# Transformer stack on one core: value products of two key tiles joined, two-bank maxima, shared semaphore clears

## The reference, cut to what matters

```
# first attention (causal, ReLU instead of softmax)
scores = einsum('bhqd,bhkd->bhqk', q, k) / sqrt(D)
att = relu(scores) * tril(ones)
att = att / (sum(att, -1) + 1e-9)
ctx = einsum('bhqk,bhkd->bhqd', att, v)
...
# second attention, beside the experts
attn = softmax(einsum('bqhd,bkhd->bhqk', q, k) / sqrt(hd), -1)
attn_out = einsum('bhqk,bkhd->bqhd', attn, v)
return attn_out + moe_out
```

## Time and profile before

| | us |
|---|---|
| median of three runs | 2062.03 |
| the profiled execution | 2057.7 |
| span of that execution (first to last instruction) | 2055.7 |
| first attention, line 885 first to last start | 324.3 to 514.9 |
| second attention, first maximum matmul to the end | 1573.7 to 2055.7 |

### The profile page before, as it was taken

The page is one execution under the profiler, slowest core; times in us unless marked ns, Lnnn a source line. Parts: engine busy times, 40 slices in busy tenths (PEclk is TensorE's granted clock), DMA queues, the critical chain, the costliest instruction groups (busy, mean ns, idle before and its releaser), DMA issues. The chain is left out here.

```text
span 2055.7 us, 36446 instructions
## 1 busy us (share of the span) xinstructions
PE 1875.9 (91%) x10746; PEld 1173.4 (57%) x10746; DVE 1491.7 (73%) x4145; ACT 937.9 (46%) x2116; POOL 981.3 (48%) x1657
## 2 busy tenths in 40 slices
PE   6997998999899999799998798799797999999997
PEld 5885773333688888577776332688573233333332
DVE  3334896777477777699997587677666889988981
ACT  1112564556122212444443344455451477777777
POOL 3554564555333333233332111388545666666662
PEclk9998998999899999999999898799997799999999
DMA  4331668786100000893000200277765444443320
GB/s 136 116 115 32 166 168 205 153 169 126 47 1 1 1 1 1 326 413 158 1 1 3 65 10 11 60 183 197 205 209 141 94 97 100 100 104 92 91 60 27
DMA packets 241226, 215.01 MB, mean 105 GB/s; under 512 B 117210, under 2 KB 215548, under 8 KB 240924
## 3 DMA queue, kind: packets, MB, share of 16 engines
q1 hardware_dynamic: 231404, 186.56, 34.3%
q0 software_dynamic: 9648, 26.36, 4.0%
HBM read 108.04 MB, written 103.12 MB: 103 GB/s over the span
## 5 line engine op out<-in xcount | busy, mean ns | idle before, releaser
L3051 DVE TENSOR_REDUCE attend_mx<-ps 128x1 f32<-128x512 f32 x512 | 321.0, 681 | 37.0 <-PE ps L2705 33.2
L2848 ACT ACTIVATE attend_w<-ps 128x512 f32<-128x512 f32 x512 | 280.6, 597 | 95.0 <-PE ps L2719 87.3
L2705 PE MATMUL ps<-keep_x,keep_o 96*128 96x512 bf16 x512 | 209.0, 414 | 6.3 <-DVE attend_mx L3051 4.5
L2719 PE MATMUL ps<-keep_o,keep_x 99*128 99x512 bf16 x512 | 191.5, 383 | 2.7 <-ACT attend_w L2848 2.7
L2705 PEld LDWEIGHTS ps<-keep_x,keep_o 96*128 96x128 bf16 x512 | 50.1, 98 | 192.2 <-DVE attend_mx L3051 145.5
L981 POOL TENSOR_TENSOR keep_early<-keep_early,first_causal 128x128 f32<-128x128 f32 x256 | 113.3, 458 | 86.0 <-ACT keep_early L949 85.0
L1003 DVE SCALAR_TENSOR_TENSOR keep_early<-ps,first_causal 128x512 f32<-128x512 f32 (+3 forms) x256 | 113.8, 485 | 47.4 <-PE ps L885 43.1
L949 ACT ACTIVATE keep_early<-ps 128x512 f32<-128x512 f32 (+3 forms) x256 | 98.7, 437 | 85.1 <-PE ps L885 84.9
L1216 PE MATMUL ps<-mlp_zT,keep_early 128*128 128x128 f32 x1056 | 129.2, 282 | 8.0 <-ACT mlp_zT L1258 8.0
L2737 PE MATMUL ps<-attend_w,keep_early 128*17 128x512 f32 x1024 | 135.5, 598 | 0.0
L1216 PEld LDWEIGHTS ps<-mlp_zT,keep_early 128*128 128x128 f32 x1056 | 122.9, 195 | 16.0 <-ACT mlp_zT L1258 16.0
(11 more groups left out here) (399 smaller groups left out, 4406.7 us busy)
## 6 DMA issues: line engine op xcount, KB each, us to landing
sorted<-keep_x SPq DMA_DIRECT2D x3, 14720.0 KB, 75.1
tok_xin<-in_xk SPq DMA_DIRECT2D x64, 256.0 KB, 2.6
qk_parts<-qkv_parts SPq DMA_DIRECT2D x33, 384.0 KB, 3.2
qk_parts<-moe_parts SPq DMA_DIRECT2D x32, 384.0 KB
sorted<-moe_zn POOLq DMA_DIRECT2D x69, 128.0 KB, 2.5
keep_o<-qk_parts SPq DMA_DIRECT2D x16, 384.0 KB, 4.5
keep_x<-qk_parts SPq DMA_DIRECT2D x16, 384.0 KB, 5.6
moe_zs<-sorted SPq DMA_DIRECT2D x45, 128.0 KB, 2.5
```

The costliest lines, as they stand in the source:

```text
L2705: nc.tensor.matmul(ps[:, MX + i % RING, :], qs[0:R, x.buf(0), h, t * P:(t + 1) * P], ks[0:R, x.buf(0), h, :], start=True, stop=True).then_ ...
L2719: nc.tensor.matmul(ps[:, SC + i % RING, :], ks[:, x.buf(2), HG * g + j, kt * P:(kt + 1) * P], qs[:, x.buf(2), HG * g + j, :], start=True, ...
L2848: nc.scalar.activation(w[:, j, kt % 2, :], ps[:, SC + (HG * k + j) % RING, :], ACT.Exp)\
L3051: nc.vector.tensor_reduce(mx[:, t, k:k + 1], ps[:, MX + (TB * k + t) % RING, :], AX, ALU.max)\
```

## The change

1. **Causal attention.** `w` holds all four key tiles (`weighed`), scores go round five banks (0, 1, 2, 3, 7), and the order of PE is new: scores 0, class values, `turn` of two groups back, scores 1, values 2 and 3 of the group before, scores 2, scores 3, values 0 and 1. `take` stands after `weigh` of tile 1, `divide` (now two groups back, its four products one instruction) after the same.
2. **Second attention.** Exponentials go to two pairs of tiles (`w_a`, `w_b`), and in even steps PE issues the values of two steps. In slots 0 and 1, whose score banks are unused, maxima go round six banks and DVE reduces two at once. The three subtractions for `side` move from DVE to POOL (`class_sides`), the last addition to `h` from POOL to DVE.
3. **End of the experts.** SP stores the last 10 blocks instead of 4, and their landing is awaited in the next stage.
4. **Clears.** Seven areas hand their semaphores on (`owes`), and the next one that pays (`owed`) clears them too: four clears and barriers are left of eleven.

```diff
@@ Area
     def clear(self):
-        if self.used:
-            self.nc.clear_and_free_semaphores(self.used)
+        if self.owes is not None:
+            self.owes += self.used
+        elif self.used:
+            self.nc.clear_and_free_semaphores(self.used + list(self.owed))
...
@@ pass_causal, PE
-                    past(pe, s_p[j] if j % 2 else s_relu[j], q)
-                    nc.tensor.matmul(ps[:, j, kt * P:S], ...
+                    last_q, last_j = divmod(HG * q + j - len(BANKS), HG)
+                    past(pe, s_p[last_j] if last_j % 2 else s_relu[last_j], last_q + 1)
+                    nc.tensor.matmul(ps[:, bank_of(q, j), kt * P:S], ...
...
+            for n in range(NG * B):
+                scores(b, g, 0)
+                class_value(b, g)
+                if n >= 2:
+                    turn(n - 2)
+                scores(b, g, 1)
+                if n >= 1:
+                    values((n - 1) // NG, (n - 1) % NG, 2)
+                    values((n - 1) // NG, (n - 1) % NG, 3)
+                scores(b, g, 2)
+                scores(b, g, 3)
+                values(b, g, 0)
+                values(b, g, 1)
@@ pass_causal, ACT
+                weigh(n // NG, n % NG, 0)
+                weigh(n // NG, n % NG, 1)
+                if n >= 1:
+                    take((n - 1) // NG, (n - 1) % NG)
+                weigh(n // NG, n % NG, 2)
+                weigh(n // NG, n % NG, 3)
@@ pass_experts
-    LAST = 4
+    LAST = LAST_BLOCKS          (10)
...
-            sp.wait_ge(s_last, 16 * LAST)
@@ pass_attend, SP, ACT and POOL
+            sp.wait_ge(env.s_last, 16 * LAST_BLOCKS)
@@ pass_attend, PE
-                        if j == 3:
+                        if j == 3 and k % 2 == 0:
                             if k and x.has(2):
+                                values(x.n(2), x.half(2), x.buf(2), k - 2)
                                 values(x.n(2), x.half(2), x.buf(2), k - 1)
                             if k == 0 and x.follows():
+                                values(x.n(3), x.half(3), x.buf(3), STEPS - 2)
                                 values(x.n(3), x.half(3), x.buf(3), STEPS - 1)
@@ pass_attend, ACT
-                        past(act, s_pv, q - 1)
+                        past(act, s_pv, q - 3)
@@ pass_attend, DVE
+                        if x.s < 2:
+                            if t % 2:
+                                dve.wait_ge(s_msc, MAXIMA * x.n(0) + at + 1)
+                                bank = (MAXIMA * x.s + at - 1) % (2 * RING)
+                                nc.vector.tensor_reduce(mx[:, t - 1:t + 1, k], ps[:, bank:bank + 2, :], AX, ALU.max).then_inc(s_mx, 2)
```

More of the change, by code:

```diff
@@ L829, in pass_causal @@
 def pass_causal(nc, env, io):
-    a = Area(nc, "causal")
+    a = Area(nc, "causal", owes=env.owed)
     ps = env.ps
@@ L915, in turn @@
                 for t in range(TB):
-                    last = nc.tensor.transpose(ps[:, 6, t * P:(t + 1) * P], ctx[:, g % 2, t * P:(t + 1) * P],
+                    last = nc.tensor.transpose(ps[:, 6, t * P:(t + 1) * P], ctx[:, n % 2, t * P:(t + 1) * P],
                                                env.ident[:, :])
                 last.then_inc(s_t, 1)
-            def batch(b, first=False):
-                for g in range(NG):
-                    for kt in range(TB):
-                        scores(b, g, kt)
-                        if kt == 2:
-                            if g:
-                                turn(b, g - 1)
-                            elif not first:
-                                turn(b - 1, NG - 1)
-                        if g or kt:
-                            values(b, g if kt else g - 1, kt - 1 if kt else TB - 1)
-                        elif not first:
-                            values(b - 1, NG - 1, TB - 1)
-                        if kt == 0:
-                            class_value(b, g)
-            batch(0, first=True)
-            for b in range(1, B):
-                batch(b)
-            values(B - 1, NG - 1, TB - 1)
-            turn(B - 1, NG - 1)
+            for n in range(NG * B):
+                b, g = n // NG, n % NG
+                scores(b, g, 0)
[10 more added lines that the diff above has]
+                values(b, g, 1)
+            values(B - 1, NG - 1, 2)
+            values(B - 1, NG - 1, 3)
+            turn(NG * B - 2)
+            turn(NG * B - 1)
         @block.scalar
@@ L2703, in max_scores @@
                     pe.wait_ge(s_load[x.buf(0)], LOADED * (x.turn(0) + 1))
-                past(pe, s_mx, MAXIMA * x.n(0) + (i - RING + 1 if i >= RING else (-1, 0, 0)[i]))
-                nc.tensor.matmul(ps[:, MX + i % RING, :], qs[0:R, x.buf(0), h, t * P:(t + 1) * P], ks[0:R, x.buf(0), h, :],
+                if x.s < 2:
+                    at = MAXIMA * x.s + i
+                    past(pe, s_mx, (at - 2 * RING) // 2 * 2 + 2)
+                    bank = at % (2 * RING)
+                else:
+                    first = (60, 60, 64) if x.s == 2 else [MAXIMA * x.n(0) + n for n in (-1, 0, -2)]
+                    past(pe, s_mx, MAXIMA * x.n(0) + i - RING + 1 if i >= RING else first[i])
+                    bank = MX + (i + 1) % RING
+                nc.tensor.matmul(ps[:, bank, :], qs[0:R, x.buf(0), h, t * P:(t + 1) * P], ks[0:R, x.buf(0), h, :],
                                  start=True, stop=True).then_inc(s_msc, 1)
@@ L2803, in _ @@
             end = Slot(UNITS - 1)
+            values(end.n(0), end.half(0), end.buf(0), STEPS - 2)
             values(end.n(0), end.half(0), end.buf(0), STEPS - 1)
@@ L2900, in class_weights, with class_sides @@
                 pool.sem_inc(s_took, 1)
+            def class_sides(x):
+                pool.wait_ge(s_mm, x.n(1) + 1)
+                pool.sem_inc(s_took, 1)
+                rows = bass.ds(TB * x.b(1), TB)
+                at = E + x.half(1) * HALF
+                for r, n in GROUPS:
+                    last = nc.gpsimd.tensor_tensor(
+                        side[:, :, r:r + HALF * n].rearrange("p t (a h) -> p t a h", a=n),
+                        env.cs[:, rows, at:at + HALF].rearrange("p t (a h) -> p t a h", a=1).to_broadcast([P, TB, n, HALF]),
+                        mm[:, :, :].rearrange("p t (a h) -> p t a h", a=1).to_broadcast([P, TB, n, HALF]), ALU.subtract)
+                last.then_inc(s_nm, 1)
             ORDER = list(range(1, NT)) + [0]
```

146 lines of the change are left out of this document (73 added, 73 removed).

## The result

The changed kernel takes 2094.74 us (median of 4 runs, 2092.32 to 2098.07) against 2063.45 us of the kernel before on the same chip: ratio 1.0156, 95% interval 1.0139 to 1.0172, so 31 us slower. The forecast was +15, and its range ended at 2094. A second series of runs gave 1.0147 (1.0130 to 1.0164). The profiled execution of the changed kernel took 2092.32 us, its span is 2090.5.

A forecast was written before the change was run, and what follows sets the result against it. PE was taken to set the pace in both attentions, with DVE close behind. The terms 9.0 + 15.8 - 4.3 - 2.6 - 2.9 = +15.0 us, added to the 2062.0 median, gave 2077 us, range 2043 to 2094.

The forecast's parts named there:

- The first attention: Causal attention: the bank wait outweighs the saving from joined bursts, +9.0 us end to end, bounds -13.5 and +14.
- the two joined bursts: Causal group on PE: two burst entries and exits fewer save 2 x 0.21 = 0.42 us per group.
- the wait for the banks: Causal group: tile 3's scores wait for reads of tile 2, eight matmuls on five banks, 0.7 us per group.
- the layout: Both attentions: one period laid out instruction by instruction per engine; before the change 5.84 us per group, 27.19 per slot.
- has some 10 us free in a slot: Second attention: POOL, 17.35 us busy per slot, has room for the `side` subtractions that PE's transposes await.
- is worth next to nothing: Second attention: moving the `side` subtractions to POOL frees 0.4 us of DVE per slot; undone, the layout is 0.7 longer.
- slots 0 to 2 together are 3 us shorter: Start of the second attention: two-bank reductions at 1.14 us instead of 1.20, PE up to six banks ahead; 3 us saved.
- The steady slot: Second attention: waits around joined bursts exceed the 0.8 us saved; slot 28.42 against 27.19 us, +1.2, over 14 slots.
- the maxima's ring: Second attention: three-bank ring, at most 1.8 us of DVE work, runs dry during a joined burst of 1.94 us.
- Clears and ends: End of the experts -4.3 us, end of the kernel -2.6, six fewer clears -2.9; together -9.8.
- The bursts pay: Rival, both attentions: rings don't run dry, PE remains the bound; -39 us, 2023 us, chance 0.13.
- Worse than laid out: Rival: five-bank wait costs 14 us, second attention 20, POOL's drain is not shortened; +28, 2090 us, chance 0.12.

The follow-up runs named there:

- side_on_dve: Changed kernel with the three subtractions for `side` back on DVE at the end of each slot; ratio to the kernel before 1.0124.
- merged: Kernel before with joined clears, changed ends, last addition on DVE, plus two-bank maxima and four weight tiles in the second attention; ratio 0.9933.
- half_maxima: Changed kernel with DVE's maxima from slot 2 on over 256 of 512 columns and exponentials of scaled scores; ratio to the kernel before 1.0126.
- ends_only: Kernel before with only joined clears, SP storing the experts' last ten blocks, and the last addition on DVE; ratio 0.9945.
- scores_between: Changed kernel with the first attention's PE order scores 2, values 0, values 1, scores 3; ratio to the kernel before 1.0102.
- after_again: The changed kernel unaltered, run once more on the chip of the follow-up series; ratio to the kernel before 1.0147.

## Why the prediction missed, and what in it held

**The first attention, +9.0 forecast, +7.2 in the trace: right in mechanism, nearly right in size.** The group came out at 6.17 forecast and 6.18 measured, and both of its causes were shown by moving them: `take` out of the way gave 5.87, the second burst between the scores 5.60. By these runs the two joined bursts saved 5.91 - 5.60 = 0.31 per group, where I had 0.42, and the wait for the banks cost 6.18 - 5.60 = 0.58, where I had 0.7: both terms were too large, and that their difference came out right is in part luck. The stage as a whole is 1.8 under the forecast, 0.5 of it because group 3 waits for image 1's loads before the change (6.38 us) and not after; the rest is in the layout's first and last groups.

**The start of the second attention: wrong, and this is the miss.** For slots 0 to 2 together I forecast -3. The lead grew by 11.6 and slot 2 by 0.6, so +12.2 in the trace. Two steps failed. First, I wrote that POOL "has some 10 us free in a slot", and that moving the `side` subtractions there "is worth next to nothing". The first is true of a steady slot (17.35 busy) and false of slots 0 and 1. The layout left out POOL's two memsets at the opening, and so the backlog in which `side` had to queue. They stand in the trace of the kernel before:

```profile
1575.69 3.51 POOL L2940 MEMSET attend_vb<- 72x4096 bf16 x1 [0.16 <-POOL attend_v0p L2937]
1579.26 13.75 POOL L2941 MEMSET keep_x<- 3x16384 bf16 x1
```

PE waited 16.67 us for `side` behind them, and with `side` back on DVE the lead was 11.2 shorter (`side_on_dve`). Second, "slots 0 to 2 together are 3 us shorter": paired maxima do shorten slots 0 and 1, by 4.7 to 5 us with `side` on DVE, but the first score waits for `nparts`, the end of the same POOL chain; `merged` shows that nothing of it is left.

**The steady slot, +1.2 forecast, +1.5 measured: right in direction, too small.** What joining saves was there, and more was lost in waits. My layout had 0.96 for the maxima's ring (28.42 to 27.46, put on record with `half_maxima`), the chip 0.70. The waits for the class row's chains, which my text only named for line 2775 and for `take`, are 1.05 after the change. Over the 13 slots 3 to 15 this is 19.9 us instead of some 16.

**The last two slots.** I counted them at the steady rate, some 2.5 in all; they grew by 5.6. Joined bursts cost 1.75 in slot 16 and 1.1 in slot 17 without any maxima, and another 2.7 where PE's clock fell in slot 16 (below).

**Clears and ends, -9.8 forecast.** `ends_only` measured -11 as a whole, its trace -7.2 up to the attention and -2.6 at the tail, for 7.2 (with all clears) and 2.6 forecast. So the sum is right; its parts are less sure. On DVE the end of the experts alone became 2.9 shorter in the changed kernel and 3.5 in `ends_only`, for 4.3 forecast, and what a clear is worth was not measured by itself. SP was the one late next in both places, as forecast; its ten stores took 10.20 us, for 10.8 laid out from the earlier trace rows.

**The whole.** Between the two spans lie 34.8 us, for 15.0 forecast. Of these 19.8 some 15 lie in slots 0 to 2, some 4 in slots 3 to 15 and 3 in the last two; the first attention and the ends give 2 back. One slip of arithmetic changes nothing: 553 to 686 ns for 128 columns is 1.04 ns per column, not 1.06.

**The rivals.** "The bursts pay" was wrong for this order, yet `scores_between` shows that joined bursts do save time where no ring is in the way, 0.16 per join instead of 0.21. "Worse than laid out" (2090) came nearest to the number, but by a mechanism that isn't the one measured: the five-bank wait did not cost more, nor was POOL's drain kept, and the second attention was 37.7 longer up to its last score, where that rival had 20. No rival had `side` waiting on POOL. The Trainium skill, TensorEngine Tiling, section PSUM Bottleneck, which the prediction took for the second attention, is borne out in part: with DVE's reads cut to 0.42 us the slot lost 0.70 of the 1.70.

## What to carry to other kernels

An engine's slack is that of the stretch in which the work is put: read its list from the stage's first instruction on, openings too, before something that another engine waits for is queued there. Joining bursts saves their entry price, but everything that a ring or a chain of other engines must do in the meantime has to fit between two joined bursts; move what stands between, before joining. When a stage gets shorter, ask which engine's chain sets its next step, since the gain may stop at a wait that was hidden.

## What the runs showed of the hardware

**A POOL fill holds some DVE operations until it ends.** The two one-input operations from SBUF to SBUF on DVE took 4.27 and 4.21 us beside a fill of 13.75 us and ended with it; in pieces of 1.8 us they took 1.60 and 1.54, alone 0.17. The `TENSOR_TENSOR` with two inputs ran beside the same fill in 0.32 for two, and so did the maxima from PSUM ahead of the two, 4 in 4.61 us. The three maxima issued behind the held operations ended with them, at 1584.83. The Trainium skill, SBUF — State Buffer, section Who interferes with whom, says that DVE in a 2-port mode (copies and tensor_scalar among them) and GpSimd lock each other out for a whole instruction, and that a two-input operation of DVE contends only with a GpSimd instruction that reads SBUF. These rows agree on the first, and on the second so far as the fill, which only writes, left the `TENSOR_TENSOR` alone.

**PE's clock falls in some executions of one and the same order.** In slots 16 and 17 no maxima run, and with joined bursts PE has pauses there. Three stretches of the changed kernel's slot 16 (columns as above; the granted clock is the third number from the end):

```profile
2042.00:2046.90 4.90, 3.37 (x16) 1.14 (x12) 0.00 (x0) 4.56 (x10) 4.11 (x5) 0.84 0.04 8
2046.90:2052.50 5.60, 5.60 (x24) 1.14 (x24) 0.00 (x0) 2.68 (x7) 3.35 (x5) 0.53 0.16 47
2052.50:2062.00 9.50, 8.26 (x54) 2.63 (x56) 2.13 (x6) 7.07 (x14) 2.86 (x4) 1.00 0.17 56
```

In 4.9 us of which PE was busy 3.37, the clock fell to near the 1.2 GHz level and a joined burst took 3.5 us instead of 1.8. In `after_again` the same 4.9 us before the same burst have PE busy for the same 3.37, and the clock stays at 1.00. Of the eight profiles with joined bursts in the second attention, slot 16 was 2.7 to 2.8 us longer in three and slot 17 by 1.6 to 1.7 in two others; in the eight with single bursts both slots had the same length to 0.01 us. Why it comes in one execution and not in the next stays open.

**POOL's drain behind its own DMAs kept its length** wherever I read it (6.69, 7.01 and 7.17 us behind stores, 6.23 and 6.25 behind indirect loads), however long the other engines took.
